# Routing walk of a graph layer: gathers with a bound on the row number, and source numbers above it for edges without a destination node

## What is computed

```python
x = x + _L0_gnn_ref(_layernorm(x, axis=-1), edge_index, ...)
x = x + _L0_ffn_ref(_layernorm(x, axis=-1)[None], ..., L0_ffn_edge_index)[0]

# in _L0_ffn_ref, with M = 6250 nodes, HEADS = 4, NUM_EXPERTS = 4
h = (x_flat @ W_gat).reshape(M, HEADS, NUM_EXPERTS)
a_src = (h * att_src).sum(-1)
a_dst = (h * att_dst).sum(-1)
e = jax.nn.leaky_relu(a_src[src] + a_dst[dst], negative_slope=0.2)
e_max = jax.ops.segment_max(e, dst, num_segments=M)
ee = jnp.exp(e - e_max[dst])
denom = jax.ops.segment_sum(ee, dst, num_segments=M)
msg = h[src] * alpha[:, :, None]
agg = jax.ops.segment_sum(msg, dst, num_segments=M)
```

## Time and profile before

| | |
|---|---|
| median of 3 runs | 4069.05 us |
| the profiled execution: span from first to last instruction | 5874.6 us |
| its own time | no time is given for it beside the span |
| PE / DVE / ACT / POOL busy, share of the span | 67% / 59% / 43% / 44% |
| routing walk in the trace, first gather to last `val` | 3740.4 to 5734.7 us |
| attention walk in the trace, first to last message | 399.5 to 3539.4 us |

### The profile page before, as it was taken

The page is one execution under the profiler, slowest core; times in us unless marked ns, Lnnn a source line. Parts: engine busy times, 40 slices in busy tenths (PEclk is TensorE's granted clock), DMA queues, the critical chain, the costliest instruction groups (busy, mean ns, idle before and its releaser), DMA issues. The chain is left out here.

```text
span 5874.6 us, 106076 instructions
## 1 busy us (share of the span) xinstructions
PE 3912.2 (67%) x26108; PEld 2753.9 (47%) x26109; DVE 3464.7 (59%) x9273; ACT 2543.2 (43%) x6305; POOL 2589.4 (44%) x2723
## 2 busy tenths in 40 slices
PE   7857777777777777777777773355666666666550
PEld 3335555555555556555555563233434343443330
DVE  8856666666666666666666668434444444444348
ACT  4445555555555555554555555223333333333320
POOL 3244444444444444444445441444444444445540
PEclk9978888888888888888888885577877787777765
DMA  6455555555555555555556555111111111111117
GB/s 212 147 163 165 155 168 163 163 161 168 156 159 163 161 168 156 165 158 165 154 166 172 159 150 177 44 15 18 21 19 21 19 21 19 22 18 19 20 21 263
DMA packets 367690, 683.50 MB, mean 116 GB/s; under 512 B 70294, under 2 KB 240482, under 8 KB 367074
## 3 DMA queue, kind: packets, MB, share of 16 engines
q0 software_dynamic: 157888, 427.05, 27.9%
q1 hardware_dynamic: 183106, 223.68, 11.5%
q10 hardware_dynamic: 26080, 25.70, 1.5%
HBM read 588.41 MB, written 87.78 MB: 115 GB/s over the span
## 5 line engine op out<-in xcount | busy, mean ns | idle before, releaser
L746 POOL DMA_INDIRECT KV<-kv_d,src_i x1564 | 1482.7, 948 | 1677.7 <-DVE msg L839 1232.4
L1389 POOL DMA_INDIRECT re_src<-src_tab_d,rsrc x1024 | 974.5, 952 | 978.7 <-SPq L1399 675.7
L1013 PE MATMUL agg_ps<-msg,oh 128*128 128x264 f32 x3512 | 1085.8, 455 | 229.7 <-issue 218.4
L1013 PEld LDWEIGHTS agg_ps<-msg,oh 128*128 128x128 f32 x3512 | 744.4, 222 | 414.2 <-issue 282.7
L1597 PE MATMUL ex_y_ps<-ex_w,ex_hid 128*112 128x256 f32 x1792 | 586.6, 461 | 301.6 <-issue 299.1
L966 PE MATMUL Q<-q,ohT 128*128 128x256 bf16 x5328 | 753.0, 297 | 15.6 <-issue 13.9
L839 DVE TENSOR_TENSOR msg<-KV,weigh_ps 128x1056 f32<-128x1056 f32 x439 | 545.7, 1243 | 268.6 <-ACT weigh_ps L920 250.1
L1516 ACT COPY re_ohT<-re_ohT_ps 128x1024 bf16<-128x1024 bf16 x179 | 181.0, 1011 | 1075.0 <-remote 1010.6
L966 PEld LDWEIGHTS Q<-q,ohT 128*128 128x128 bf16 x5328 | 531.4, 105 | 117.4 <-issue 19.5
L909 ACT ACTIVATE square<-iota_b,off 128x128 bf16<-128x128 bf16 x1784 | 569.2, 392 | 0.3
L1597 PEld LDWEIGHTS ex_y_ps<-ex_w,ex_hid 128*112 128x112 f32 x1792 | 363.7, 214 | 434.1 <-issue 366.0
(11 more groups left out here) (264 smaller groups left out, 6199.0 us busy)
## 6 DMA issues: line engine op xcount, KB each, us to landing
q<-q_d SPq DMA_DIRECT2D x446, 192.0 KB
y_d<-ex_y ACTq DMA_DIRECT2D x56, 448.0 KB
rg_ye<-y_d SPq DMA_DIRECT2D x7, 3584.0 KB, 11.8
KV<-kv_d,src_i POOLq DMA_INDIRECT x1564
nu_xs<-xs_d SPq DMA_DIRECT2D x7, 2688.0 KB, 11.9
re_src<-src_tab_d,rsrc POOLq DMA_INDIRECT x1024
kv_d<-pr_kv SPq DMA_DIRECT2D x49, 260.0 KB, 2.2
xs_d<-pr_xs SPq DMA_DIRECT2D x49, 256.0 KB, 2.4
```

The source lines that it names most:

```text
L746: pool.indirect_dma_start(out=KV[:, t % (KVR * G), :], out_offset=None, in_=k.kv_d, in_offset=bass.IndirectOffsetOnAxis(ap=k.src_i[:, t:t ...
L1013: m = pe.matmul(agg_ps[:, 0:HEADS * HW], oh32[ring(s, 2)][:, t, :], msg[ring(s, 2)][:, t, :, :].rearrange("p h e -> p (h e)"), start=False ...
L1389: pool.indirect_dma_start(out=gs[:, t % (RING * RG), :], out_offset=None, in_=k.src_tab_d, in_offset=bass.IndirectOffsetOnAxis(ap=k.rsrc[: ...
```

## The change

It has three parts. In `prepare`, VectorE makes 8192 of every destination of 6250 or more and 0 of the others (in `dst_i`, no longer needed), and adds that to `rsrc`, so that the source numbers of these edges lie at 8192 or above. In the routing walk each gather carries a bound, 6271: a number above it is no error, and its row is not transferred. Since such rows of `gs` then keep what stood there, POOL sets `gs` to zero once, and waits for that before it gathers; the wait uses `ring_seen`, a semaphore that POOL raises and nobody else waits for.

```diff
@@ prepare, vector @@
                 d.on(v.tensor_scalar(k.rsrc[:, :], bits, SRC_MASK, None, ALU.bitwise_and))
+                d.on(v.tensor_scalar(dst_i[:, :], dst_i[:, :], N, 1 << SRC_BITS, ALU.is_ge, ALU.mult))
+                wait()
+                d.on(v.tensor_tensor(k.rsrc[:, :], k.rsrc[:, :], dst_i[:, :], ALU.add))
                 v.wait_ge(ok["tab_products"], 4)
@@ route_experts, gpsimd @@
                 pool.iota(part[:, :], ...).then_inc(ok["constants"], 1)
+                pool.memset(gs[:, :, :], 0.0).then_inc(ok["ring_seen"], 1)
                 pool.wait_ge(ok["max_in"], 1)
                 pool.partition_all_reduce(peak[:, 1, :], peak[:, 0, :], P, bass.bass_isa.ReduceOp.max).then_inc(ok["max"], 1)
+                pool.wait_ge(ok["ring_seen"], 1)
...
                             pool.indirect_dma_start(out=gs[:, t % (RING * RG), :], out_offset=None, in_=k.src_tab_d,
-                                                    in_offset=bass.IndirectOffsetOnAxis(ap=k.rsrc[:, t:t + 1], axis=0)).then_inc(gathered[h % 4], 16)
+                                                    in_offset=bass.IndirectOffsetOnAxis(ap=k.rsrc[:, t:t + 1], axis=0),
+                                                    bounds_check=NPAD - 1, oob_is_err=False).then_inc(gathered[h % 4], 16)
```

## The result

The change makes the kernel slower: 4120.5 us (median of 4 runs, 4118.71 to 4123.87) against 4068.07 us for the kernel before (4 runs, 4067.04 to 4070.93), a ratio of 1.0129 with a 95% interval of 1.0115 to 1.0143, or +52 us. The forecast was 4034 us, faster; the measured time is that of the slower rival with 46 ns a gather (4120 us).

The account below looks back on a forecast made before the run. POOL's gather rate was taken to bound the routing walk in a run. From 4069 us, 38 us saved there and 3.4 us added on VectorE gave 4034 us; overall range 3985 to 4140 us, the forecast's own 4010 to 4055.

Parts of the forecast that it names:

- the slower rival: Routing walk: the bound is paid on all 1024 gathers and POOL bounds; 4120 us at 46 ns each; chance 0.33.
- The stalls of the trace: Long steps in both walks, such as 17.43 us in routing, were taken as the profiled execution's own.
- The sum of a run from parts: Parts outside the routing walk, without stalls, sum to 2795 us; 4069 less that leaves 1274 us for the walk.
- The attention step: Attention walk: 4.69 us from one message to the next where nothing stalls, 438 times, 2054 us.
- POOL's gather rate bounds the walk: Routing walk in a run: 1024 gathers at 1.252 us plus 4.7 us, 1287 us, 32 to 45 above the steps.
- the step chain: Routing walk: 15.3 us to the first `val`, then 175 steps of 7.01 us mean, 1242 us.
- The bound lies in just the groups whose rows the change skips: Routing walk's last 30 groups: POOL needs 10.0 us a group against steps of 7.0; before them POOL keeps up.
- c, the price of a dead gather: POOL, 243 dead gathers: 0.78 us each, between 1.252 and 0.30; 1.07 suffices for the walk's whole 38 us gain.
- The other reading: Skill page's SWDGE comparison: a GpSimd core computes one descriptor pair per operation, so a dead gather's price falls with rows.
- d, taken as 0: POOL, each of 1024 gathers: added price of the bound's register move and comparing, taken as 0; every unhidden 8 ns costs 8 us.
- VectorE +3.4 us: End of preparation: compare and multiply 1.16 us plus 32-bit add 2.2 us, fully exposed; range 2.4 to 3.6.
- POOL's memset 0: Start of routing walk: a 1.6 us memset hidden in POOL's idle time, 0 us; otherwise 1.6 us once.

Follow-up runs that it names:

- the two kernels that gather less: Kernel before with no gather for the 30 groups of dead rows alone: 4009.77 us; the same with the bound on the 784 gathers left: 4015.3 us.
- the sizes tried: Kernel before with the ring's memset, gathers of 128, 64, 32 and 16 rows in turn: 4043.74 us without the bound, 4055.92 us with it.
- the kernel without the bound: Changed kernel with no bound on its gathers, the two VectorE operations and the memset kept, the sum put in an unread tile: 4074.46 us, ratio 1.0006.

## Why the prediction was wrong

- **The stalls of the trace are not a run's: right.** The second profile of the same kernel spans 4071.5 us. The sum of a run from parts gave 1274 us for the walk; it is 1307. The attention step was right (4.69 us, measured (2421.4 - 372.1) / 438 = 4.68); the start was not: I took 399.5 us up to the first message from the stalled trace, and it is 372.1.
- **POOL's gather rate bounds the walk, the step chain would be 1242 us: right.** Shown by the two kernels that gather less; without the dead groups the stretch is 1242.2 us. That the figure is exact is partly luck: a step is 7.1 us in the first part and 6.6 in the last, not 7.01 throughout. The worth of relieving POOL was 63 us, not 38, since the walk before is 1307 us and not 1274 to 1287. I had the rate at 1.252 us; it is 1.271, with the gap as I took it (0.305) and a mean gather of 966 ns, where the stalled trace has 952.
- **"The bound lies in just the groups whose rows the change skips": wrong.** VectorE waits there, but POOL is busy from the first group on, and the bound on the first half alone costs 21 us.
- **The step that failed first: c, the price of a dead gather, taken as the middle between 1.252 and 0.30 us.** It is 0.997 + 0.30 = 1.297 us, as a live one, and with it the 38 us of gain fall away. I chose a middle between ends far apart and needed only 0.18 us of saving; the earlier trace rows held the warning, two gathers of 128 rows with equal price at 26 times the bytes. The Trainium skill, DMA: Bandwidth & Descriptors, section "Anatomy of one DMA — SWDGE (gpsimd) path", calls descriptor generation "small, variable"; the sizes tried agree with that as to what a row adds: 0.93 ns on average, beside 826 ns for the gather itself. The other reading that the prediction set beside it, a descriptor pair per operation and so a c that falls with the rows, takes every row for an operation, which no run shows; at 0.93 ns a row c would fall by 0.12 us at most. The sign that I gave for the saving, packets down by a quarter, failed too.
- **The step that gave the size: d, taken as 0.** The evidence of the earlier trace rows was about the sequencer, and there it held: the register move of 29 ns left the gap at 0.30 us. The price came inside the gather, which I had named as the part that no row shows: 50 ns in the median, 43 ns in the mean (966 to 1009), and 1024 x 0.043 = 44 us.
- **VectorE +3.4 us, POOL's memset 0:** 2.3 and 0.9 us (the expectation for the kernel without the bound still has 3.0, from the start of the attention walk). The add over 2048 halves takes 1.23 us, as one pass of 1024 would, the end of the bounds that I didn't take. That the memset might push the reduction back stood in the prediction as its second reading, priced at 1.6 us.
- **The slower rival, 4120 us:** right in place and mechanism. That the time is met to 1 us is chance: its 46 ns came from a register instruction on another engine's queue and met 43 to 50 ns inside the gather, and its 3.4 us for VectorE stand for 2.3 + 0.9.

## What to carry to other kernels

A bound on an indirect gather made the rows' bytes vanish and left the time on the issuing engine; where that engine's rate is the bound, skip whole gathers by a branch, not rows. When a profiled span is far from the time of a run, take a second profile before arguing from its waits; here the median durations and the dispatch gaps of the two profiles agreed, and the mean gather did not (952 and 966 ns). An engine without idle time pays for every added nanosecond in the whole stretch, even if its consumer only waits at the end.

## What the runs showed of the hardware

- A gather of 128 rows with a bound held POOL for 997 ns, without for 947 ns; at 16 rows 880 and 841 ns. Ahead of each stood a gap of 0.305 us.
- Rows above the bound were not left out of the queue: in the windows shown, as many packets (5984) moved 0.11 MB instead of 1.93 and took 1.8% instead of 9.7% of the DMA engines' time. In the DMA records of that trace a live gather is 16 packets of 640 bytes (8 rows each) and 16 of 4 bytes; with every row above the bound the 640 become 32.
- A gather was lengthened, from 947 ns up to 1.2 us and more, almost only where VectorE's `val` ran beside it (55 of the 58 over 1.09 us, in the second trace of the kernel before).
- Two profiled executions of one kernel spanned 5874.6 and 4071.5 us. What made the first slow was not tried.
- What the 39 ns a gather are spent on, why 13 ns more come at 128 rows only, and what in VectorE's work lengthens a gather, stays open.
